# A pair pass on a grid of 128 edges, with the attributes laid out turned

## The chip, the cores and the metric

The kernel runs on one core of one Trainium2 chip. The metric is the device time of one launch in microseconds, as the median of several runs. Beside it there is one profiled execution, from which all rows below are taken.

## The reference, cut to what matters

Four graph layers run one after another on a graph of N = 6250 nodes and E = 106250 edges, sorted by destination; the width is D = 128. Layers 0 (two graph attentions), 1 and 3 (graph convolutions) are not changed in what they compute. The changed part is mainly layer 2:

```python
pos_e = x_feat[src] + edge_attr
v = jax.nn.gelu(pos_e @ W1.T + b1, approximate=False) * bases
aggr = jax.ops.segment_sum(v, dst, num_segments=n_nodes)
```

`edge_attr` and `bases` are two arrays of 106250 x 128 floats. The kernel computes `pos_e @ W1.T + b1` as a table row `x_feat @ W1.T + b1`, gathered by `src`, plus `edge_attr @ W1.T`.

## The kernel before, in words

The nodes stand in NB = 49 blocks of P = 128 (the partition count). A tile is 128 edges that follow each other in the sorted list. The tile tables (`tile_tables`, L485 to L656) give each block as many tiles as its edges fill, rounded up: a block's first tile begins at that block's first edge, so the last tile of a block also reads some edges of the next block, which are masked because their place in the block (`LOCAL`) is 128 or more. The number of tiles is fixed at TILES = 880, in GROUPS = 220 groups of GT = 4. Counted on the input's destination list, 854 tiles have edges of their own; the other 26, at the end, are padding: their edge number is clamped to E, where the padded source list holds zeros, so all 128 rows that such a tile gathers are one and the same row.

Three stages gather by `SRC` for all 880 tiles, one indirect DMA per tile, issued by POOL in `gather` (L1026, recorded under L1033) into a ring of DEEP = 12 groups: the logits of the two attention layers (`gat_logits`) and the pair pass. At the end of each logits stage POOL also issues 16 scatters that add edge weights to an adjacency matrix in DRAM (`merge`, L1114); the first groups of scatters each wait for the landing of the one before. Gathers and scatters use the same POOL queue. Every stage ends with a barrier of all engines, in which POOL drains.

`pair_pass` (L1620) does, per group of 4 tiles: SP fetches 4 x 128 KB of attributes and bases into a ring of 6 groups (L1651, one DMA per tile, starting at the tile's first edge); POOL gathers the 4 x 128 table rows; PE turns the attributes (4 transposes, L1660); ACT copies them from PSUM (L1667); PE multiplies with the weights (L1675); DVE adds the gathered rows (`sum_up`, L1684); ACT applies gelu (L1688); DVE multiplies with the bases (L1694) and builds 4 one-hot matrices (L1045); PE multiplies one-hot and values (L1708); DVE adds 4 products, each to its block of the accumulator (L1063). All PSUM buffers are pairs, the value ring V has 4 places. The order of the instructions on each engine is that of the list in `pipeline`, which says how many groups a piece runs behind the gather: products 4, additions 5. Each engine works through its list in order; semaphores tie them.

In `sort_edges` (L284) SP loads the destination list twice to SBUF and copies the source, destination and weight lists inside DRAM, each as one flat transfer (L301); the copies must be there only at the end of that stage. In `tile_tables` a chain of small DVE operations computes where each tile begins; when it is known POOL fetches 21 windows of edges (L588), and DVE turns them into masks and keys.

## Time and profile before

| what | value |
|---|---|
| median of 3 runs | 6823.73 us (6820.1 to 6828.18) |
| the profiled execution's own time | 6820.84 us |
| its span in the trace | 6819.0 us |
| mean granted TensorE clock | 0.843 |
| pair pass, first gather to next stage | 4237 to 5370 us |
| first logits stage, gathers | 161 to 1285 us |
| second logits stage, gathers | 2001 to 3125 us |

Engines are PE (matmul), PEld (its weight loads), DVE, ACT, POOL and SP. A row of a group of instructions gives the count, the busy time, the mean duration of one and the idle time of the engine just before them with what ended it; "issue" is a wait that the profile shows no releaser for. Times in a timeline are from the start of the span.

### The profile page before, as it was taken

What the parts mean: (1) busy time and instruction counts of PE and PEld (TensorE: products, weight loads), DVE (VectorE), ACT (ScalarE), POOL (GpSimd) and SP (SyncE); (2) the same over time, 40 slices, a digit from 0 to 9 for tenths busy, and PEclk for the clock granted to TensorE, in tenths of its full rate; (3) what the DMA queues carried; (4) which work ended last, traced back from release to release, by engine and by line L of the source; (5) the groups of instructions that cost most, each with busy time, mean ns of one, the idle gap of its engine ahead of it and who ended that gap; (6) DMA issues with size and microseconds to landing.
All of it is one profiled execution on the core that took longest, in us unless ns stands there. A gap on an engine that the chain in (4) does not pass through costs nothing. (4 is left out here: it accounts for less than half of the span.)

```text
span 6819.0 us, 113163 instructions
## 1 busy us (share of the span) xinstructions
PE 5493.8 (81%) x30494; PEld 4417.2 (65%) x30494; DVE 3783.5 (55%) x13003; ACT 2171.3 (32%) x7007; POOL 4607.1 (68%) x4391
## 2 busy tenths in 40 slices
PE   2988998538769999885886996666666699999998
PEld 2777787536667777774775995665666455555555
DVE  6555562288975555223887445666666644344343
ACT  4333334268943333333995003222222300000000
POOL 1777677678857777777886661777777267276473
PEclk9777678678967777876997998888888799999999
DMA  6888875656734444335444884555555489899997
GB/s 217 256 276 277 261 214 160 116 104 138 142 68 102 105 103 105 80 80 54 77 76 117 287 288 139 165 157 157 158 158 157 79 289 307 287 305 299 302 304 256
DMA packets 903995, 1231.39 MB, mean 181 GB/s; under 512 B 230601, under 2 KB 640861, under 8 KB 890407
## 3 DMA queue, kind: packets, MB, share of 16 engines
q1 hardware_dynamic: 607544, 887.00, 41.0%
q0 software_dynamic: 207392, 219.55, 17.9%
q10 hardware_dynamic: 88428, 117.57, 5.1%
q8 instruction: 256, 4.19, 0.3%
q14 instruction: 375, 3.07, 0.1%
HBM read 987.45 MB, written 237.38 MB: 180 GB/s over the span
## 5 line engine op out<-in xcount | busy, mean ns | idle before, releaser
L1033 POOL DMA_INDIRECT ACC<-table,TABS x1760 | 1696.9, 964 | 628.2 <-issue 603.0
L1348 POOL DMA_INDIRECT BUF<-table,TABS x840 | 799.3, 952 | 581.6 <-issue 245.6
L1114 POOL DMA_INDIRECT adjacency<-TABS x600 | 966.9, 1612 | 311.5 <-issue 260.2
L1033 POOL DMA_INDIRECT BUF<-table,TABS x880 | 841.5, 956 | 331.5 <-issue 331.5
L1805 PE MATMUL picked<-ident,ACC 128*128 128x128 f32 (+1 forms) x3520 | 890.7, 345 | 0.0
L1804 PE MATMUL picked<-G,OH 128*128 128x128 f32 (+1 forms) x2352 | 619.6, 356 | 203.9 <-DMA ACC<-table,TABS 110.8
L2185 PE MATMUL asum<-BUF 128*128 128x144 f32 x3520 | 561.2, 305 | 165.6 <-DVE BUF L2163 162.6
L1805 PEld LDWEIGHTS picked<-ident,ACC 128*128 128x128 f32 (+1 forms) x3520 | 673.2, 222 | 0.0
L1804 PEld LDWEIGHTS picked<-G,OH 128*128 128x128 f32 (+1 forms) x2352 | 431.6, 218 | 342.1 <-issue 315.8
L1708 PE MATMUL sums<-BUF,G 128*128 128x128 f32 x1760 | 320.0, 339 | 399.0 <-DVE ACC L1063 398.7
L2185 PEld LDWEIGHTS asum<-BUF 128*128 128x128 f32 x3520 | 476.4, 197 | 196.4 <-issue 182.1
L1825 PEld LDWEIGHTS lcol<-attT,BUF 128*128 128x128 f32 (+1 forms) x3520 | 539.3, 232 | 55.7 <-issue 49.8
L2131 ACT ACTIVATE BUF<-iota_row,TABS 128x128 f32<-128x128 f32 x1760 | 555.1, 386 | 23.5 <-PEq L89 23.5
L1708 PEld LDWEIGHTS sums<-BUF,G 128*128 128x128 f32 x1760 | 277.7, 240 | 435.5 <-issue 435.2
L1825 PE MATMUL lcol<-attT,BUF 128*128 128x8 f32 (+1 forms) x3520 | 545.7, 278 | 2.7 <-ACT BUF L1843 2.7
L1817 DVE TENSOR_TENSOR BUF<-BUF,picked 128x512 f32<-128x512 f32 (+1 forms) x440 | 298.0, 678 | 406.1 <-ACT BUF L1811 404.9
L1063 DVE TENSOR_TENSOR ACC<-ACC,asum 128x144 f32 (+1 forms) x1760 | 462.7, 263 | 94.3 <-PE asum L2185 14.4
L1881 DVE SCALAR_TENSOR_TENSOR BUF<-BUF,TABS,wspread 128x128 bf16<-128x128 f32 (+1 forms) x600 | 324.4, 541 | 337.7 <-PE wspread L1864 234.3
L1831 ACT ACTIVATE ACC<-lcol 128x32 f32<-128x32 f32 (+1 forms) x440 | 81.7, 186 | 1281.5 <-PE lcol L1825 1272.8
L1783 DVE TENSOR_SCALAR G<-BUF,iota_col 128x512 f32<-128x512 bf16 x440 | 223.5, 509 | 478.6 <-DMA BUF<-locals 476.1
L1688 ACT ACTIVATE BUF<-BUF 128x512 f32<-128x512 f32 x220 | 138.6, 630 | 837.3 <-DVE BUF L1684 837.3
L1262 PE MATMUL sums<-ACC,BUF 128*128 128x128 f32 x3332 | 386.1, 276 | 23.3 <-DMA BUF<-adjacency 13.5
(397 smaller groups left out, 10318.8 us busy)
## 6 DMA issues: line engine op xcount, KB each, us to landing
TABS<-adjacency SPq DMA_DIRECT2D x272, 512.0 KB
BUF<-in_edge_pair SPq DMA_DIRECT2D x880, 128.0 KB
BUF<-adjacency SPq DMA_DIRECT2D x102, 1024.0 KB
BUF<-adjacency SPq DMA_DIRECT2D x204, 512.0 KB
adjacency<-zeros ACTq DMA_DIRECT2D x44, 1792.0 KB
G<-adjacency SPq DMA_DIRECT2D x136, 512.0 KB
kept<-ACC SPq DMA_DIRECT2D x220, 272.0 KB
G<-kept SPq DMA_DIRECT2D x220, 272.0 KB
```

The lines of the kernel that those rows point to most:

```text
L1033: po.indirect_dma_start(rows[:, slot, j, 0:width], None, tab, bass.IndirectOffsetOnAxis(ap=SRC[:, q * GT + j:q * GT + j + 1], axis=0)).the ...
L1063: ve.tensor_tensor(at, at, self.from_[:, j, 0:self.width], ALU.add).then_inc(S("added"), 1)
L1114: po.indirect_dma_start(adj_flat, bass.IndirectOffsetOnAxis(ap=PLACE[:, k:k + 1], axis=0), TOTAL[:, k:k + 1], None, compute_op=ALU.add).th ...
L1262: m = pe.matmul(sums[:, j, 0:P], RA[n % len(RA)][:, (i * w + j) * P:(i * w + j + 1) * P], xw[:, b + i, :], start=b + i == 0, stop=b + i == ...
L1348: po.indirect_dma_start(R[:, q % deep_ring, j, :], None, table, bass.IndirectOffsetOnAxis(ap=SRC[:, k:k + 1], axis=0)).then_inc(S(f"gather ...
L1708: m = pe.matmul(sums[h][:, j, :], HOTS[:, slot, j, :], V[:, q % 4, j, :], start=True, stop=True)
L1804: pe.matmul(z, XRB[q % 3][:, j, :], OHT[:, slot, j, :], start=True, stop=False)
L1805: m = pe.matmul(z, R[:, q % DEEP, j, :], ident[:, :], start=False, stop=True)
L1825: m = pe.matmul(lcol[slot % 2][:, j * H:(j + 1) * H], Z[:, q % 3, j * P:(j + 1) * P], attT[0:W, 0:H], start=True, stop=True)
L1881: ve.scalar_tensor_tensor(JUNK[:, at % 3, 0:j + 1, :], KEYS[:, n % 2, 0:j + 1, :], KEY[:, k:k + 1], wspread[:, 0:j + 1, :], ALU.is_equal, ...
L2131: ac.activation(HOT[:, slot, j, :], iota_row[:, :], ACT.Abs, scale=-1.0, bias=LOCAL[:, bass.ds(q * GT + j, 1)]).then_inc(S("gap"), 1)
L2185: m = pe.matmul(sums[slot % 2][:, j, 0:WIDE], HOT[:, slot, j, :], RHS[:, slot, j, :], start=True, stop=True)
```

## The change

1. Tiles lie on a grid: the edge list is cut into 831 cells of 128 edges, and each block gets all the cells that hold any of its edges. A cell that two blocks share appears twice, and the edges of the other block are masked, now on both sides (`LOCAL` below 0 or 128 and more). Counted on the same list, 879 of the 880 tiles have edges of their own. The loops still run over 880 tiles and 220 groups. `START` holds a cell number rather than an edge number.
2. The attribute array is laid out on the host per cell, turned to 128 features x 128 edges. The pair pass no longer turns it: `turn_attr` and `copy_attr` are gone, and `times_w` reads the fetched tile.
3. The pair pass has deeper rings: 9 groups of fetched pairs (6 before), 6 of values (4), 4 PSUM buffers each for `pre` and `sums` (2). The order is written out: sums run 4 groups behind the gather, the multiplication with the bases 5, products 6, additions 9. One-hots and additions alternate on DVE.
4. The three edge lists are copied as 128 rows of equal length each; they are padded to a multiple of 128.
5. The tile tables need more small DVE operations, and the masks of the keys and of the adjacency places (`put_aside`) one more each.
6. The path for unsorted edges (not taken here, the list is sorted) turns and turns back the attributes.

```diff
-TAIL = 2 * P
+SPREAD = 834
+TAIL = SPREAD * P - FRONT - E
 GT = 4
 RING = 4
 DEEP = 12
 SORT_T = -(-E // P)
+CELLS = SORT_T + 1
...
-                sp.dma_start(copy, given).then_inc(S("edges_copied"), 16)
+                sp.dma_start(copy.rearrange("(p c) -> p c", p=P), given.rearrange("(p c) -> p c", p=P)
+                             ).then_inc(S("edges_copied"), 16)
...
-            go(ve, lambda: ve.tensor_tensor(number[:, 0:NB], starts[:, 1:NB + 1], starts_t, ALU.subtract))
-            go(ve, lambda: ve.tensor_scalar(number[:, 0:NB], number[:, 0:NB], float(P - 1), None, ALU.add))
-            go(ve, lambda: ve.tensor_copy(number_i, number[:, 0:NB]))
-            go(ve, lambda: ve.tensor_scalar(number_i, number_i, 7, None, ALU.logical_shift_right))
-            go(ve, lambda: ve.tensor_copy(number[:, 0:NB], number_i))
+
+            def first_cell(cell, edges, plus):
+
+                go(ve, lambda: ve.tensor_scalar(number_i, edges, float(plus), None, ALU.add))
+                go(ve, lambda: ve.tensor_scalar(number_i, number_i, 7, None, ALU.logical_shift_right))
+                go(ve, lambda: ve.tensor_copy(cell, number_i))
+
+            first_cell(first, starts_t, 0)
+            first_cell(shift, starts[:, 1:NB + 1], P - 1)
+            go(ve, lambda: ve.tensor_tensor(shift, shift, first, ALU.subtract))
+            go(ve, lambda: ve.tensor_tensor(filled, starts[:, 1:NB + 1], starts_t, ALU.is_gt))
+            go(ve, lambda: ve.tensor_tensor(number[:, 0:NB], shift, filled, ALU.mult))
...
-            go(ve, lambda: ve.scalar_tensor_tensor(shift, first, float(-P), starts_t, ALU.mult, ALU.add))
+            first_cell(shift, starts_t, 0)
+            go(ve, lambda: ve.tensor_tensor(shift, shift, first, ALU.subtract))
+            go(ve, lambda: ve.tensor_scalar(shift, shift, float(P), None, ALU.mult))
...
+            go(ve, lambda: ve.tensor_scalar(cell, edge, 1.0 / P, None, ALU.mult))
...
-            go(ve, lambda: ve.tensor_scalar(real_edge, local, float(P), None, ALU.is_lt))
+            go(ve, lambda: ve.tensor_scalar(real_edge, local, 0.0, None, ALU.is_ge))
+            go(ve, lambda: ve.scalar_tensor_tensor(real_edge, local, float(P), real_edge, ALU.is_lt, ALU.mult))
...
-            PD = 6
-
-            rooms = BUF[2][:, :, :].rearrange("p b d -> p (b d)")
-            PAIR = BUF[1][:, 0:2 * PD * GT, :].rearrange("p (r t a) d -> p r t (a d)", r=PD, t=GT)
+            PD, VD, FREE = 9, 6, 4
+            SUM_LATE, BASE_LATE, PRODUCT_LATE, ADD_LATE = 4, 5, 6, 9
+
+            V = BUF[2][:, 0:VD * GT, :].rearrange("p (r t) d -> p r t d", r=VD)
+            halves_of_pairs = [BUF[1][:, 2 * GT * i:2 * GT * (i + 1), :] for i in range(PD - 3)]
+            halves_of_pairs += [BUF[2][:, VD * GT + 2 * GT * i:VD * GT + 2 * GT * (i + 1), :] for i in range(3)]
+            PAIR = [h.rearrange("p (t a) d -> p t (a d)", a=2) for h in halves_of_pairs]
             R = BUF[0][:, 0:DEEP * GT, :].rearrange("p (r t) d -> p r t d", r=DEEP)
-            EAT = rooms[:, 0:2 * GT * P].rearrange("p (r t d) -> p r t d", r=2, t=GT)
-            V = rooms[:, 2 * GT * P:6 * GT * P].rearrange("p (r t d) -> p r t d", r=4, t=GT)
-            HOTS = G[:, :, :, :].rearrange("p r t d -> p (r t d)")[:, 0:4 * GT * P].rearrange(
+            four = G[:, :, :, :].rearrange("p r t d -> p (r t d)")[:, 0:4 * GT * P].rearrange(
                 "p (r t e) -> p r t e", r=4, t=GT)
+            HOTS = [four[:, i] for i in range(4)] + [OH[:, i] for i in range(2)]
+            assert len(HOTS) == VD
...
-                turned = [psum(ps, f"turned{i}", [P, GT, P]) for i in range(2)]
-                pre = [psum(ps, f"pre{i}", [P, GT, P]) for i in range(2)]
-                sums = [psum(ps, f"sums{i}", [P, GT, P]) for i in range(2)]
-                adder = Adder(acc, sums, D, "v_free")
...
+                pre = [psum(ps, f"pre{i}", [P, GT, P]) for i in range(FREE)]
+                sums = [psum(ps, f"sums{i}", [P, GT, P]) for i in range(FREE)]
...
+                    cells = pairs.rearrange("(c p) d -> c p d", p=P)
                     for q in range(GROUPS):
                         at = nc.values_load_multi_w_load_instructions(
-                            START[0:1, bass.ds(q * GT, GT)], engines=(SP,), min_val=0, max_val=E,
-                            skip_runtime_bounds_check_because="a tile's first edge is a minimum with E")[1]
+                            START[0:1, bass.ds(q * GT, GT)], engines=(SP,), min_val=0, max_val=CELLS - 1,
+                            skip_runtime_bounds_check_because="a tile's cell is a minimum with the last one")[1]
                         wait(sp, S("based"), q - PD + 1)
                         settle(sp, "sync")
                         for j in range(GT):
-                            sp.dma_start(PAIR[:, q % PD, j, :], pairs[bass.ds(at[j], P), :]
+                            sp.dma_start(PAIR[q % PD][:, j, :], cells[bass.ds(at[j], 1), :, :].rearrange("a p d -> p (a d)")
                                          ).then_inc(S(f"pair{q % PD}"), 16)
...
-                def turn_attr(q, slot, turn):
-                    h = slot % 2
+                def times_w(q, slot, turn):
                     pe.wait_ge(S(f"pair{q % PD}"), 16 * GT * (q // PD + 1))
 
-                    wait(pe, S("attr_copied"), q - 1)
+                    wait(pe, S("summed"), q - FREE + 1)
                     for j in range(GT):
-                        m = pe.transpose(turned[h][:, j, :], PAIR[:, q % PD, j, 0:D], ident[:, :])
-                    m.then_inc(S("attr_turned"), 1)
-
-                def copy_attr(q, slot, turn):
-                    h = slot % 2
-                    ac.wait_ge(S("attr_turned"), q + 1)
-                    wait(ac, S("pre_done"), q - 1)
-                    ac.activation(EAT[:, h], turned[h][:, :, :], ACT.Copy).then_inc(S("attr_copied"), 1)
-
-                def times_w(q, slot, turn):
-                    h = slot % 2
-                    pe.wait_ge(S("attr_copied"), q + 1)
-
-                    wait(pe, S("summed"), q - 1)
-                    for j in range(GT):
-                        m = pe.matmul(pre[h][:, j, :], EAT[:, h, j, :], wmat[:, :], start=True, stop=True)
+                        m = pe.matmul(pre[q % FREE][:, j, :], PAIR[q % PD][:, j, 0:D], wmat[:, :], start=True, stop=True)
                     m.then_inc(S("pre_done"), 1)
...
-                def hots(q, slot, turn):
-                    wait(ve, S("v_free"), q - 3)
-                    for j in range(GT):
-                        m = one_hot(HOTS[:, slot], q * GT, j)
-                    m.then_inc(S("hot"), 1)
+                    ve.tensor_tensor(v, v, PAIR[q % PD][:, :, D:2 * D], ALU.mult).then_inc(S("based"), 1)
+
+                def hot(q, j):
+                    if not 0 <= q < GROUPS:
+                        return
+                    if not j:
+                        wait(ve, S("v_free"), q - VD + 1)
+                    m = one_hot(HOTS[q % VD], q * GT, j)
+                    if j == GT - 1:
+                        m.then_inc(S("hot"), 1)
 
                 def products(q, slot, turn):
-                    h = slot % 2
                     pe.wait_ge(S("hot"), q + 1)
                     pe.wait_ge(S("based"), q + 1)
-                    wait(pe, S("added"), (q - 1) * GT)
+                    wait(pe, S("added"), (q - FREE + 1) * GT)
                     for j in range(GT):
-                        m = pe.matmul(sums[h][:, j, :], HOTS[:, slot, j, :], V[:, q % 4, j, :], start=True, stop=True)
+                        m = pe.matmul(sums[q % FREE][:, j, :], HOTS[q % VD][:, j, :], V[:, q % VD, j, :], start=True, stop=True)
                     m.then_inc(S("v_free"), 1)
 
-                def add(q, slot, turn):
-                    adder.start(q, slot)
+                def add_and_hots(u):
+
+                    q = u - ADD_LATE
+                    if q >= 0:
+                        ve.wait_ge(S("v_free"), q + 1)
+                        blocks = blocks_of(DVE, q)
                     for j in range(GT):
-                        adder.tile(j)
+                        hot(u - BASE_LATE, j)
+                        if q >= 0:
+                            wait(ve, S("added"), q * GT + j)
+                            at = acc[:, bass.ds(blocks[j], 1), :].rearrange("p a d -> p (a d)")
+                            ve.tensor_tensor(at, at, sums[q % FREE][:, j, :], ALU.add).then_inc(S("added"), 1)
...
-                pipeline(nc, [(gather_rows, 0), (turn_attr, 1), (copy_attr, 1),
-                              (times_w, 2), (times_base, 3), (sum_up, 2), (gelu, 2), (hots, 2), (products, 4),
-                              (add, 5)])
+                for u in range(GROUPS + ADD_LATE):
+                    for piece, late in ((gather_rows, 0), (times_w, 1), (add_and_hots, 0), (sum_up, SUM_LATE),
+                                        (gelu, SUM_LATE), (times_base, BASE_LATE), (products, PRODUCT_LATE)):
+                        q = u - late
+                        if piece is add_and_hots:
+                            add_and_hots(u)
+                        elif 0 <= q < GROUPS:
+                            piece(q, q % RING, q // RING)
...
+                    ve.scalar_tensor_tensor(LATER[:, cols], LOCAL[:, cols], 0.0, LATER[:, cols],
+                                            ALU.is_lt, ALU.add).then_inc(S("aside"), 1)
...
-    inputs["edge_pair"] = np.concatenate([inputs.pop("edge_attr_128"), inputs.pop("edge_attr_128_n2")], axis=1)
+    attr, base = (np.pad(np.asarray(inputs.pop(name)), ((0, CELLS * P - E), (0, 0))).reshape(CELLS, P, D)
+                  for name in ("edge_attr_128", "edge_attr_128_n2"))
+    inputs["edge_pair"] = np.concatenate([attr.transpose(0, 2, 1), base], axis=2).reshape(CELLS * P, 2 * D)
```

## Rows read from the trace of the kernel before

**Rows 1.** The page, part 1: busy time, share, instructions.

```profile
...
PE 5493.8 (81%) x30494; PEld 4417.2 (65%) x30494; DVE 3783.5 (55%) x13003; ACT 2171.3 (32%) x7007; POOL 4607.1 (68%) x4391
```

**Rows 2.** Groups of instructions (busy, mean ns, idle before) of the pair pass, 4230 to 5370.

```profile
...
L1033 POOL DMA_INDIRECT BUF<-table,TABS x880 | 841.5, 956 | 331.5 <-issue 331.5
L1708 PE MATMUL sums<-BUF,G 128*128 128x128 f32 x1760 | 320.0, 339 | 399.0 <-DVE ACC L1063 398.7
L1675 PE MATMUL pre<-wmat,BUF 128*128 128x128 f32 x1760 | 303.3, 330 | 0.0
...
L1063 DVE TENSOR_TENSOR ACC<-ACC,sums 128x128 f32 x880 | 250.5, 285 | 97.0 <-DVE ACC L1063 3.3 <-PE sums L1708 0.6
L1045 DVE TENSOR_SCALAR G<-iota_row,TABS 128x128 f32<-128x128 f32 x880 | 192.6, 290 | 0.0
L1660 PE MATMUL turned<-ident,BUF 128*128 128x128 f32 x880 | 177.4, 339 | 33.2 <-DMA BUF<-in_edge_pair 33.1
L1684 DVE TENSOR_TENSOR BUF<-pre,BUF 128x512 f32<-128x512 f32 x220 | 152.1, 691 | 348.4 <-issue 279.3 <-PE pre L1675 57.5 <-DMA BUF<-table,TABS 10.9
L1694 DVE TENSOR_TENSOR BUF<-BUF 128x512 f32<-128x512 f32 x220 | 150.7, 685 | 0.7 <-issue 0.7
...
L1667 ACT ACTIVATE BUF<-turned 128x512 f32<-128x512 f32 x220 | 128.1, 582 | 54.1 <-PE turned L1660 53.4
```

**Rows 3.** Line 1033 over the whole span: ns min/median/max, first and last start.

```profile
...
L1033 POOL DMA_INDIRECT BUF<-table,TABS x880: 941/947/1347, 4237.0 to 5345.7; - x176
```

**Rows 4.** Timeline (start, us, engine, line, idle before) of the pair pass's end.

```profile
...
5345.69 0.95 POOL L1033 DMA_INDIRECT BUF<-table,TABS  x1 [0.30 <-issue]
...
5359.99 0.69 DVE L1684 TENSOR_TENSOR BUF<-pre,BUF 128x512 f32<-128x512 f32 x1 [1.31 <-issue]
...
5367.77 1.57 DVE L1063 TENSOR_TENSOR ACC<-ACC,sums 128x128 f32 x4 [0.43 <-DVE ACC L1063]
```

**Rows 5.** Line 1033 alone, 5199 to 5311.5, with time from issue to landing.

```profile
...
DMA to landing us min/median/max: 2.8/3.0/3.7
```

**Rows 6.** Line 1033 alone, 5312 to 5370.

```profile
...
L1033 POOL DMA_INDIRECT BUF<-table,TABS x28: 943/947/1319, 5311.2 to 5345.7; - x28
...
DMA to landing us min/median/max: 13.4/14.0/14.2
```

**Rows 7.** POOL's timeline, end of the first logits stage.

```profile
...
1284.18 0.94 POOL L1033 DMA_INDIRECT ACC<-table,TABS  x1 [0.31 <-issue]
1285.42 1.63 POOL L1114 DMA_INDIRECT adjacency<-TABS  x1 [0.30 <-issue]
...
1303.80 1.57 POOL L1114 DMA_INDIRECT adjacency<-TABS  x1 [11.15 <-DMA adjacency<-TABS]
...
1313.70 1.55 POOL L1114 DMA_INDIRECT adjacency<-TABS  x1 [2.74 <-issue]
...
1326.71 1.55 POOL L1114 DMA_INDIRECT adjacency<-TABS  x1 [0.30 <-issue]
```

**Rows 8.** POOL's timeline, end of the second logits stage.

```profile
...
3142.29 1.56 POOL L1114 DMA_INDIRECT adjacency<-TABS  x1 [2.06 <-DMA adjacency<-TABS]
```

**Rows 9.** DVE's timeline at the start of the tile tables.

```profile
...
48.96 0.21 DVE L504 TENSOR_TENSOR st<-st 128x49 f32<-128x49 f32 x1 [1.99 <-PEq L345]
49.21 0.19 DVE L505 TENSOR_SCALAR st<-st 128x49 f32<-128x49 f32 x1
```

**Rows 10.** DVE's timeline behind the edge windows.

```profile
...
94.24 0.64 DVE L595 CAST BUF<-BUF 128x910 f32<-128x910 int32 x1 [12.03 <-DMA BUF<-w_sorted,st]
...
107.54 1.09 DVE L619 SCALAR_TENSOR_TENSOR BUF<-BUF 128x896 f32<-128x896 f32 x1
```

**Rows 11.** Line 1893, the mask of `put_aside`.

```profile
...
L1893 DVE SCALAR_TENSOR_TENSOR TABS<-TABS x2: 435/460/486, 1024.1 to 2744.1; 128x320 f32<-128x320 f32 x1, 128x280 f32<-128x280 f32 x1
```

**Rows 12.** SP's waits, first 48 us (us in total, times, longest).

```profile
...
SPq L235 <- DVE FLAG L338: 12.7, 1, 12.7
```

**Rows 13.** POOL's groups in the second logits stage, 1995 to 3125.3.

```profile
...
L1033 POOL DMA_INDIRECT ACC<-table,TABS x880 | 856.4, 973 | 272.5 <-issue 272.5
```

More of the change, by code:

```diff
@@ L544, in tile_tables @@
             placed = st[0][:, 88:88 + TCOL]
+            cell = st[0][:, 96:96 + TCOL]
+            go(ve, lambda: ve.tensor_scalar(cell, edge, 1.0 / P, None, ALU.mult))
             go(ve, lambda: ve.tensor_scalar(scaled, blk, turn_by[:, :], None, ALU.add))
@@ L555, in tile_tables @@
                 rows = psum(ps, "rows", [1, 2, 1024])
-                for n, (col, tab) in enumerate(((blk, BLOCK), (edge, START))):
+                for n, (col, tab) in enumerate(((blk, BLOCK), (cell, START))):
                     for g in range(TCOL):
```

37 lines of the change are left out of this document (23 added, 14 removed).

## The prediction

> **What bounds the kernel now.** The page comes first: no engine is full over the span, the longest are PE at 81% and POOL at 68% [rows 1]. These are means over stages with different limits, so the change has to be read in its own stages. The largest part of it is the pair pass, and there the groups of instructions decide. DVE, PE and ACT all stand idle in it for hundreds of microseconds. POOL is the one engine that never waits for anybody: its 880 gathers take 841.5 us, and all of its idle time is "issue", 331.5 us, about 0.3 us before each [rows 2]. From the first gather at 4237.0 [rows 3] to the start of the last at 5345.69 [rows 4] lie 1108.7 us, over 879 steps 1.261 us each, or 5.05 us per group of four. DVE waits 348.4 us in front of `sum_up`, 279.3 of it under "issue" [rows 2]; a gather lands 3.0 us after its issue [rows 5], and I read this wait as the wait for the gathered rows. So this pass runs at the pace at which POOL issues.
>
> The next view is the same line in two windows. Up to 5311 a gather lands in 2.8 to 3.7 us [rows 5]; behind that in 13.4 to 14.2 us [rows 6]. The input's list gives 854 tiles with edges of their own and 26 padding tiles, whose 128 rows are one and the same row. 26 x 1.261 = 33 us before the last gather is 5313, just where landing turns slow. I take the repeated row as the cause. What follows is in the timeline: the last gather is issued at 5345.69, but its `sum_up` runs at 5359.99 and the last four additions end at 5367.77 + 1.57 = 5369.3 [rows 4]. The last timelines are those of the logits stages, which gather by the same table. There POOL goes on to scatters as soon as its gathers are issued, and its second group of scatters waits 11.15 us for the first to land, behind the slow gathers in the same queue; with ordinary landing that wait is like the next one, 2.74 us [rows 7]. In the second attention layer 2.06 us are lost the same way [rows 8].
>
> **The change, part by part.**
>
> *Transposes and copies removed.* PE is busy 320.0 + 303.3 + 177.4 = 800.7 us over 220 groups, 3.64 us per group; without the 880 transposes 2.83. ACT loses 220 copies of 0.58 us [rows 2]. Both are below POOL's 5.05 us already, so in the steady part this is worth 0. The cover is POOL's issue; were it gone, the 128.1 us of copies and 177.4 us of transposes would be the price. What is late next is the gather, as before.
>
> *DVE's new order.* A group costs 4 additions of 0.285, 4 one-hots of 0.29, 0.691 and 0.685 [rows 2]: 3.68 us at most, the same work as before. Interleaved, each addition's wait for the one before it falls behind a one-hot. 3.68 is under 5.05: worth 0 in the steady part. Behind the waiting `sum_up` on DVE now stand the bases of the group before, and the additions of a group 5 further back; with 6 places for values and 4 buffers of PSUM nobody is blocked by that.
>
> *Deeper fetch ring.* SP may run 9 groups ahead. At the start that is 36 transfers instead of 24, beside gathers that have 12 groups of room: 0.
>
> *The drain of the pair pass.* With 879 real tiles the last gather should land like those of [rows 5]: 5345.69 + 3.0 = 5348.7. `sum_up` of the last group can then start, as PE is groups ahead. Behind it DVE has, in program order: 0.69; the additions of group 215 with the last one-hots between them, 4 x (0.285 + 0.29) = 2.3; the bases, 0.69; and the additions of groups 216 to 219. Four additions in a row take 1.57 [rows 4]; with 0.3 for the register loads and waits ahead of them (estimate; the wait in that row is 0.43) 1.87 each, 7.5 in all. Sum 11.2, end at 5359.9 against 5369.3: **-9.4 us**. Bounds: 0 if the landing stays slow; -12 if the additions follow without gaps and the rows are there 1.4 us sooner.
>
> *First logits stage.* POOL's chain from 1284.18 to the last scatter (1326.71 + 1.55) sets the end, with the drain of the barrier. The wait of 11.15 becomes about 2.74 [rows 7]: **-8.4 us**. Bounds: 0, and -10.9 if it shrinks to the 0.3 of the other scatters.
>
> *Second logits stage.* 2.06 - 0.3 [rows 8]: **-1.8 us**, bounds 0 and -1.8.
>
> *Tile tables.* Ahead of the windows the DVE chain has 9 operations in place of 5, and then 5 in place of 1: 8 more. One takes 0.19 to 0.21 us, and the next starts 0.25 behind [rows 9]: 8 x 0.23 = +1.8, all on the path, for POOL's window fetch starts behind them and DVE then waits for the windows (12.03 us, [rows 10]). Behind the windows one more operation over 128x896, 1.09 us [rows 10], in a chain with no gaps: +1.1. Together **+2.9**, bounds +2 and +4. The new `cell` operation and the shift of START lie beside POOL's windows: 0.
>
> *Mask in `put_aside`.* Two more operations of 0.46 us, at about 1024 and 2744 [rows 11], in stages that POOL's gathers pace and hundreds of microseconds before anybody waits for them: 0, at most +0.9.
>
> *Edge lists as equal rows.* SP's own wait at the end of that stage is for DVE, 12.7 us [rows 12]; the copies are issued some 40 us earlier. Their form can only move the landing of the two loads issued ahead of them: 0, bounds -2 and +2.
>
> *Grid in the other stages.* The loops still have 880 tiles; 25 more gather real rows instead of one row, 25 fewer scatter nothing but padding. Outside the three stages above nothing waits on these: 0, bounds -3 and +3. (The first logits stage has waits on its `kept` ring that may fall otherwise.)
>
> Sum: -9.4 - 8.4 - 1.8 + 2.9 = -16.7 us. Against the profiled execution's own 6820.84 that gives 6804.1; the median of the runs shown, 6823.73, lies 2.9 above it, and the median is what is asked for: **6807 us**, -0.25%.
>
> *A rule that speaks against it.* POOL's gathers in the pair pass last 0.941 to 1.347 us, their mean is 0.956 against a median of 0.947 [rows 2, 3]: something stretches a few of them. The Trainium skill (SBUF — State Buffer, "Who interferes with whom") says that DVE and GpSimd share a port pair which one of them holds for a whole instruction, that `tensor_scalar` can take it in its two-port modes, and that POOL's descriptor writing is then locked out. The one-hots are such instructions, and the change spreads them over more of DVE's time. By that rule the sum would be worse; by the row, in which 880 one-hots at 0.29 us already lie beside the gathers, the cost is 9 ns a gather. It is the second rival below, priced from rows.
>
> **The rivals.**
>
> 1. *The slow landing is not the padding's doing* (it comes, say, with the end of a list, and stays). For: the trace shows when, not why. Against: it starts where the padding starts, in all three stages that gather by this table [rows 6, 7, 8]. Then the last rows are there at about 5359.7, the drain behind them takes 11.2, the pair pass ends 1.6 later than now, and the waits of the logits stages stay: 6823.7 + 2.9 + 1.6 = 6828.
> 2. *One-hots between the additions stretch POOL's gathers.* Place: the pair pass; price: 880 times the growth of the mean; it decides from 16.7/880 = 19 ns on, a mean of 975 instead of 956. The gathers of the second logits stage, beside other DVE work, have 973 [rows 13], so such a mean occurs. At 1.00 us it would be +38.7: 6807 + 39 = 6846, slower than before. Against: number, shapes and durations of DVE's operations in the pass are the same as now.
> 3. *Only the pair pass gains* (the scatters of the first logits stage wait for something else, such as the zero fill of the adjacency or each other): 6807 + 8.4 + 1.8 = 6817. For: the wait is named after the scatters' own landing. Against: the next one in the row is 2.74 only.
> 4. *The pair pass was paced by the loop over PE, ACT and DVE, and POOL's constant 0.3 hides that*: then 5.05 us per group would fall to about 4.2, 220 x 0.85 = 187 us less, 6620. Against: the ring of 12 groups would have to be full and POOL's waits would show a releaser and vary; they do not.
>
> **How the numbers follow.** Forecast 0.65; rival 1 0.12; rival 2 0.08; rival 3 0.12; rival 4 0.03. Between the forecast's own bounds (each term's bounds taken together as unlikely to fall on one side at once) it lies at 6797 to 6816. Two executions of this kernel differ by up to 8 us, 0.1%; 0.2%, 13.6 us, is about what a measurement can tell from no change, so "faster" means below 6810.1. Of the forecast's 0.65 some four fifths lie there, 0.51, and rival 4's 0.03: 0.54. Slower by over 0.2% is rival 2, 0.08. Within 0.2% is what is left, the upper fifth of the forecast's range and rivals 1 and 3: 0.38. The range takes in the forecast's bounds and rival 3, and stops short of rivals 1, 2 and 4: 6795 to 6822.
>
> **What the new profile would show.** Right: POOL's gathers in the pair pass still 1.25 to 1.27 us apart with 0.3 of "issue" before each; landing near 3 us to the end in all three gathering stages; last `sum_up` about 3 us behind the last gather; about 11 us from there to the end of the pass; the first wait of the second group of scatters 2 to 3 us; PE less busy in the pair pass by some 180 us with no effect on its length; the first gather of the first logits stage about 3 us later than now. Wrong: landings of 14 us at the end (rival 1), a mean gather over 975 ns (rival 2), a wait of 11 us before the fifth scatter (rival 3), or gathers of the pair pass closer than 1.25 us (rival 4).

## The result and the profile after

The changed kernel takes 6840.73 us (median of 20 runs, 6825.09 to 6865.56), the kernel before 6826.02 us beside it (20 runs, 6811.87 to 6844.63). The ratio is 1.0022, with an interval of 1.0013 to 1.0031. It is slower by 9 to 21 us, where -16.7 us were forecast. The profiled execution took 6833.4 us, its span is 6831.6, against 6819.0. Two executions of one kernel differ by more than the 8 us that the prediction took from three of them: the 20 of the kernel before spread over 33 us.

The gathers of the pair pass show where. First the same groups as in [rows 2] (busy us, mean ns, idle before), 4210 to 5384 of the changed kernel:

```profile
L1060 POOL DMA_INDIRECT BUF<-table,TABS x880 | 885.5, 1006 | 331.4 <-issue 331.4
...
L1736 DVE TENSOR_TENSOR ACC<-ACC,sums 128x128 f32 x880 | 250.7, 285 | 4.1 <-issue 1.4 <-DVE ACC L1736 0.8
...
L1696 DVE TENSOR_TENSOR BUF<-pre,BUF 128x512 f32<-128x512 f32 x220 | 152.1, 692 | 509.9 <-DMA BUF<-table,TABS 478.3 <-PE pre L1688 19.1 <-PE sums L1722 9.3
L1706 DVE TENSOR_TENSOR BUF<-BUF 128x512 f32<-128x512 f32 x220 | 150.9, 686 | 0.0
```

L1060 is the gather (L1033 before), L1696 `sum_up` (L1684), L1706 `times_base`, the multiplication by the bases (L1694), L1736 the additions (L1063). POOL still waits for nobody: the idle time under "issue" is what it was, 331.4 us. But a gather lasts 1006 ns on the mean, in place of 956: 44.0 us over 880. The line alone over the whole span, to be set against [rows 3]:

```profile
L1060 POOL DMA_INDIRECT BUF<-table,TABS x880: 941/947/1466, 4216.2 to 5368.8; - x176
```

The median is 947 ns in both. So not every gather got slower, some did by much: 135 are over 1.1 us, 17 before. From the first gather to the last are 1152.6 us, 1108.7 before: +43.9. The pair pass begins 20.8 us earlier and its last gather starts 23.1 us later.

(Below, a gather that `times_base` lengthens is called held.) A timeline from the middle of the pass (start, duration, engine, line, idle before) shows one long gather and what lies beside it:

```profile
4739.90 0.69 DVE L1696 TENSOR_TENSOR BUF<-pre,BUF 128x512 f32<-128x512 f32 x1 [2.40 <-DMA BUF<-table,TABS]
4740.51 0.68 DVE L1706 TENSOR_TENSOR BUF<-BUF 128x512 f32<-128x512 f32 x1
...
4740.70 1.31 POOL L1060 DMA_INDIRECT BUF<-table,TABS  x1 [0.30 <-issue]
4741.11 0.28 DVE L1072 TENSOR_SCALAR G<-iota_row,TABS 128x128 f32<-128x128 f32 x1
...
4742.31 0.94 POOL L1060 DMA_INDIRECT BUF<-table,TABS  x1 [0.30 <-issue]
4743.56 0.95 POOL L1060 DMA_INDIRECT BUF<-table,TABS  x1 [0.30 <-issue]
```

`times_base` starts at 4740.51, the gather 0.19 us later, and it lasts 1.31 us. The three gathers that follow lie beside one-hots and additions and last 0.94 and 0.95. I sorted all 880 by the time from the start of the last `times_base` to their own start:

```
                       0-100   100-200  200-300  300-400  400-500 ns  all others
changed: gathers          39        62       27       17        4         731
         mean ns        1309      1356     1261     1162     1053         947
before:  gathers           0         5        8        3       10         854
         mean ns           -      1325     1257     1120     1062         950
```

All 135 long gathers are in the first five columns, in which 149 start; before, all 17, and 26 start there. From 100 ns on, the later a gather starts in `times_base` the shorter it is, one for one: a long gather ends 1.50 us behind the start of that instruction, 0.82 behind its end. (In the first column 29 of the 39 are long.) 142 of the 149 are third gathers of their group. The reason is in the new order. `times_base` now stands directly behind `sum_up`, and `sum_up` is released by the fourth gather's landing (the wait of 478.3 us in the group above); 0.6 us later `times_base` starts, and POOL's next gather, the third of the following group, starts 0.72 us behind `sum_up` at the median. POOL and DVE beat in one rhythm, so this meeting repeats in about two groups of three. Before, `times_base` stood ahead of `sum_up`, 2.88 us behind the last one, between two starts.

The other terms came. The timelines of the ends, for [rows 7] and [rows 4] (first POOL at the end of the first logits stage, then POOL's last gather of the pair pass, then DVE behind it):

```profile
1284.10 0.94 POOL L1060 DMA_INDIRECT ACC<-table,TABS  x1 [0.30 <-issue]
...
1294.69 1.57 POOL L1141 DMA_INDIRECT adjacency<-TABS  x1 [2.12 <-DMA adjacency<-TABS]
...
1304.15 1.55 POOL L1141 DMA_INDIRECT adjacency<-TABS  x1 [2.30 <-issue]
...
1317.16 1.55 POOL L1141 DMA_INDIRECT adjacency<-TABS  x1 [0.30 <-issue]
```

```profile
5368.80 0.94 POOL L1060 DMA_INDIRECT BUF<-table,TABS  x1 [0.30 <-issue]
```

```profile
5372.85 0.69 DVE L1696 TENSOR_TENSOR BUF<-pre,BUF 128x512 f32<-128x512 f32 x1 [3.55 <-DMA BUF<-table,TABS]
...
5382.02 1.58 DVE L1736 TENSOR_TENSOR ACC<-ACC,sums 128x128 f32 x4 [0.25 <-DVE ACC L1736]
```

The last gathers of the pass, 5335 to 5395, against [rows 6]:

```profile
L1060 POOL DMA_INDIRECT BUF<-table,TABS x28: 943/947/1024, 5334.9 to 5368.8; - x28
...
DMA to landing us min/median/max: 2.5/2.5/2.6
```

The landing of 14 us is gone, and with it the wait of 11.15 us behind the first group of scatters (now 2.12).

### The profile page after: what moved, and what is told of

Its sections match the earlier page's. It is cut to its first block and busy times, and to the rows that moved or that the text cites. A ratio compares the mean times of both kernels' runs of the same rounds, so it can differ in the third digit from the quotient of the medians.

```text
span 6831.6 us, 110756 instructions
## 1 busy us (share of the span) xinstructions
PE 5435.8 (80%) x29614; PEld 4345.1 (64%) x29614; DVE 3749.6 (55%) x13015; ACT 2060.7 (30%) x6787; POOL 4653.3 (68%) x4391
## 3 DMA queue, kind: packets, MB, share of 16 engines
q0 software_dynamic: 207392, 219.55, 16.6%
## 5 line engine op out<-in xcount | busy, mean ns | idle before, releaser
L1060 POOL DMA_INDIRECT ACC<-table,TABS x1760 | 1697.1, 964 | 626.5 <-issue 602.5
L1375 POOL DMA_INDIRECT BUF<-table,TABS x840 | 799.7, 952 | 573.2 <-issue 247.1
L1060 POOL DMA_INDIRECT BUF<-table,TABS x880 | 885.5, 1006 | 331.4 <-issue 331.4
L1688 PE MATMUL pre<-wmat,BUF 128*128 128x128 f32 x1760 | 360.2, 369 | 497.7 <-DVE BUF L1696 463.3
L2215 PE MATMUL asum<-BUF 128*128 128x144 f32 x3520 | 547.1, 299 | 170.6 <-DVE BUF L2193 167.7
L1688 PEld LDWEIGHTS pre<-wmat,BUF 128*128 128x128 f32 x1760 | 310.5, 265 | 545.1 <-issue 508.8
L1696 DVE TENSOR_TENSOR BUF<-pre,BUF 128x512 f32<-128x512 f32 x220 | 152.1, 692 | 509.9 <-DMA BUF<-table,TABS 478.3
```

The lines of the kernel that those rows point to most:

```text
L1060: po.indirect_dma_start(rows[:, slot, j, 0:width], None, tab, bass.IndirectOffsetOnAxis(ap=SRC[:, q * GT + j:q * GT + j + 1], axis=0)).the ...
L1375: po.indirect_dma_start(R[:, q % deep_ring, j, :], None, table, bass.IndirectOffsetOnAxis(ap=SRC[:, k:k + 1], axis=0)).then_inc(S(f"gather ...
L1688: m = pe.matmul(pre[q % FREE][:, j, :], PAIR[q % PD][:, j, 0:D], wmat[:, :], start=True, stop=True)
L2215: m = pe.matmul(sums[slot % 2][:, j, 0:WIDE], HOT[:, slot, j, :], RHS[:, slot, j, :], start=True, stop=True)
```

## The experiments

Theory B: a gather that starts in the first half microsecond of `times_base` is held until that instruction ends; the change put `times_base` where a gather mostly starts. Rival H is the rival 2 of the prediction: the one-hots between the additions. A further rival is that rings, layout or grid do it. Last, the granted clock is 0.831 in the profile of the changed kernel and 0.843 in that of before; runs 1 and 4 have 0.831 as well and are faster than the kernel before, so the clock doesn't make the loss.

The runs fell on two kinds of chip. On the first kind (two chips) the kernel before takes 6827 to 6833 us beside the runs, on the second kind (three others) 8166 to 8169. Only on the first kind does POOL set the pace of the pair pass (section 9), so only there does a time speak of the loss. Ratios are always to the kernel before, measured beside the run. In the edits, "..." marks what is left out.

Runs 1 to 4 are on the first kind.

### 1. `times_base` in the middle of the one-hots and additions (changed kernel)

```
-    ... (gelu, SUM_LATE), (times_base, BASE_LATE), (products, PRODUCT_LATE)):
+    ... (gelu, SUM_LATE), (products, PRODUCT_LATE)):
...
     for j in range(GT):
+        if j == 2 and 0 <= u - BASE_LATE - 1 < GROUPS:
+            times_base(u - BASE_LATE - 1, 0, 0)
         hot(u - BASE_LATE, j)
```

> The changed kernel, with one edit: the multiplication by the bases no longer follows sum_up directly but stands between the second and the third pair of one-hot and addition, some 0.8 us later. Theory B (a gather that starts in the first half microsecond of the multiplication is held up by it; in the changed kernel the third gather of a group always does): the multiplication now starts 1.4 us behind sum_up, where no gather starts; mean gather of the pair pass 945 to 955 ns instead of 1006, time 6841 - 880 x 0.053 = 6794 us (6788 to 6802). Rival H (one-hots between the additions stretch the gathers): the one-hots alternate as before, mean stays 1000 to 1010 ns, 6841 us.

Measured: 6802.6 us, ratio to before 0.9974 (0.9963 to 0.9985). The gathers, as the page has them:

```profile
L1060 POOL DMA_INDIRECT BUF<-table,TABS x880 | 843.2, 958 | 331.3 <-issue 331.3
```

48 ns less, and nothing else was moved. Mean and time are just above what I expected (by 3 ns and 0.6 us): the phase moves with the edit, and 52 gathers still start in the first 500 ns of `times_base`, 26 of them at 400 to 500 where the hold is 0.12 us. All 27 over 1.1 us are among the 52. B holds, H falls as the cause of the loss: the alternation is unchanged.

### 2. One-hots and additions in blocks again (changed kernel)

```
     for j in range(GT):
         hot(u - BASE_LATE, j)
+    for j in range(GT):
         if q >= 0:
             wait(ve, S("added"), q * GT + j)
```

> The changed kernel with the four one-hots in a row and then the four additions in a row, as in the kernel before; the multiplication by the bases stays directly behind sum_up. Theory B: nothing changes, mean gather 1000 to 1010 ns, 6838 to 6846 us. Rival H: mean gather back to 956 ns, 6797 us.

Measured: 6840.06 us, ratio 1.0018 (1.0004 to 1.0032).

```profile
L1060 POOL DMA_INDIRECT BUF<-table,TABS x880 | 883.8, 1004 | 331.3 <-issue 331.3
```

Again 149 gathers in the first 500 ns, 132 over 1.1 us. The alternation is worth nothing, either way, as the prediction had it.

### 3. `times_base` inside the one-hots (kernel before)

```
     for j in range(GT):
+        if j == 2 and q > 0:
+            times_base(q - 1, 0, 0)
         m = one_hot(HOTS[:, slot], q * GT, j)
     ...
+    if q == GROUPS - 1:
+        times_base(q, 0, 0)
...
-    (times_w, 2), (times_base, 3), (sum_up, 2), ...
+    (times_w, 2), (sum_up, 2), ...
```

> The kernel before, with one edit: the multiplication by the bases stands between the second and the third one-hot behind sum_up, instead of ahead of sum_up. Theory B: it then starts 1.0 us behind the start of sum_up, and the third gather of a group starts at 1.16 us: held up, mean gather 990 to 1015 ns instead of 956, time 6826 + 880 x 0.045 = 6866 us (6850 to 6880). Rival H: no one-hot stands between additions, mean 956, 6826 us.

Measured: 6828.18 us, ratio 1.0004 (0.9991 to 1.0016); mean gather 954 ns. A miss, and H's number. The trace shows why: with `times_base` no longer ahead of it, `sum_up` starts at another point of POOL's rhythm. The third gather starts 0.73 us behind `sum_up` at the median, not 1.17, so ahead of `times_base` at 1.0. Only 7 gathers start in its first 500 ns. A gather that starts ahead of it isn't held (in the changed kernel 24 gathers start within 100 ns ahead of it, with a mean of 946 ns); the one exception that I found is here, a gather that starts 0.14 us ahead of it at 4264.45 and lasts 1.65 us. I had taken the phase for fixed, and it moves with the edit. The trace also shows that H's mechanism exists, though it is small: 245 other gathers start in the first 200 ns of a one-hot here, with a mean of 969 ns, against 944 of those that start beside additions. That is about 6 us over the pass, and most of why the mean is 954 with almost nothing held. It also says where `times_base` must stand for a hold: at 0.6. That is run 9.

### 4. The same place and length, but one operand in PSUM (changed kernel)

```
-    ac.activation(V[:, q % VD], V[:, q % VD], ACT.Gelu)
+    ac.activation(pre[q % FREE][:, :, :], V[:, q % VD], ACT.Gelu)
-    ve.tensor_tensor(v, v, PAIR[q % PD][:, :, D:2 * D], ALU.mult)
+    ve.tensor_tensor(v, pre[q % FREE][:, :, :], PAIR[q % PD][:, :, D:2 * D], ALU.mult)
     ... # and times_w waits for "based" of q - FREE in place of "summed"
```

> The changed kernel, in its own order, but the gelu is written to PSUM, so that the multiplication by the bases reads one operand from PSUM and one from SBUF; same length, same place, same result. Theory B in its narrow form (it is the two operands in SBUF that hold a gather up): mean gather about 946 ns, time 6841 - 880 x 0.060 = 6788 us (6780 to 6798). Theory B in its wide form (any DVE instruction of 0.68 us in this place does): stays at 1000 to 1010 ns, 6841 us. Rival H: also 1000 to 1010 ns, 6841 us.

Measured: 6794.2 us, ratio 0.9962 (0.9947 to 0.9977).

```profile
L1060 POOL DMA_INDIRECT BUF<-table,TABS x880 | 831.3, 945 | 331.4 <-issue 331.4
```

```profile
4742.39 0.68 DVE L1706 TENSOR_TENSOR BUF<-pre,BUF 128x512 f32<-128x512 f32 x1
```

`times_base` is as long as it was, 0.68 us, and directly behind `sum_up`; 111 gathers start in its first 500 ns, with a mean of 944 ns, and none of the 880 is over 1.02 us. So it is not any DVE instruction of this length in this place that holds them: with both operands in SBUF it does, with one in PSUM it doesn't. (The edit also moves the gelu's output out of SBUF; run 1 leaves the gelu as it was and loses the holds by the place alone.) `sum_up` reads a pair of PSUM and SBUF as well, and holds none: in the changed kernel 37 gathers start in its first 500 ns, the longest of 948 ns.

### 5. `times_base` as four instructions (changed kernel)

```
-    ve.tensor_tensor(v, v, PAIR[q % PD][:, :, D:2 * D], ALU.mult)
+    for j in range(GT):
+        m = ve.tensor_tensor(v[:, j], v[:, j], PAIR[q % PD][:, j, D:2 * D], ALU.mult)
     ...
```

> The changed kernel, with the multiplication by the bases in its place but as four instructions over 128x128 instead of one over 128x512, all with both operands in SBUF. If a gather is held until the instruction ends that runs when it starts, the longest hold is a quarter as long: gathers of 1.0 to 1.2 us in place of 1.3 to 1.45, mean 950 to 975 ns, 6841 - 880 x 0.045 = 6801 us (6792 to 6815). If it is held until DVE has no such instruction left, the mean stays at 1000 ns or more, 6841 us.

The second and the third run of it:

> The changed kernel with the multiplication by the bases as four instructions over 128x128, once more, for the same reason. Held until the instruction ends: gathers of 1.0 to 1.2 us at most, mean 950 to 975 ns, 6801 us (6792 to 6815). Held until DVE has no such instruction left: mean 1000 ns or more, 6841 us.

> The changed kernel with the multiplication by the bases as four instructions. In the two runs on the other chip no gather was over 1.09 us, with a mean of 957 ns. Where POOL paces the pass this gives 6841 - 880 x 0.049 = 6798 us (6790 to 6808); if the holds come more often when the phase locks, up to 6815.

Three runs, all on the second kind of chip: ratios 1.0011 (0.9999 to 1.0023), 1.0003 (0.9992 to 1.0013), 0.9994 (0.9982 to 1.0006) there. Its time says nothing (below), its gathers do. From the second run, the timeline and the line's min/median/max:

```profile
5523.58 0.89 DVE L1707 TENSOR_TENSOR BUF<-BUF 128x128 f32<-128x128 f32 x4
...
5524.02 1.08 POOL L1060 DMA_INDIRECT BUF<-table,TABS  x1 [0.30 <-DVE BUF L1696]
```

```profile
L1060 POOL DMA_INDIRECT BUF<-table,TABS x880: 942/947/1085, 5096.7 to 6482.7; - x176
```

In none of the three is a gather over 1.09 us, though 190 to 200 start within 500 ns behind the start of one of the four; the means are 957, 957 and 950 ns, as expected. That holds do occur on this kind of chip is shown by run 6. The gather above starts in the third of the four instructions (each of 0.28 us; they start at 5523.58, 5523.78, 5523.98 and 5524.19) and ends 0.83 us behind that one's end, as the long ones of the changed kernel do. A gather is held to the end of the one instruction that runs when it starts and then goes on, though another follows.

### 6. The padding's rows made different (kernel before)

```
+            if name == "src":
+                a[-tail:] = np.arange(tail) * 37 % N
```

> The kernel before, in whose padding of the list of source rows 256 different rows stand instead of row 0 256 times; nothing else is changed. If the repeated row is what makes the last gathers land in 14 us, they now land in about 3: behind the last gather the pair pass ends 9 us sooner, the first logits stage 9 us, the second 2 us: 6827 - 20 = 6807 us (6802 to 6812). If the slow landing comes with the end of a list, 6827 us.

The second to the fourth run of it:

> The kernel before with 256 different rows in the padding of the list of sources, once more, for the same reason. On a chip like the first: landing of the last gathers about 3 us, pair pass, first and second logits stage end 9, 9 and 2 us sooner behind their last gather, 6827 - 20 = 6807 us (6802 to 6812); if the slow landing comes with the end of a list, 6827 us.

> The kernel before with 256 different rows in the padding. Where POOL paces the gathers: from the last gather to the end of the stage 9 us less in the pair pass and in the first logits stage, 2 us less in the second, 6807 us (6802 to 6812); if the repeated row is not the cause, 6827 us.

> The kernel before with 256 different rows in the padding. Where the kernel before takes 6827 to 6833 us: from the last gather to the end of the stage 9 us less in the pair pass and in the first logits stage, 2 us less in the second, 20 us in all, 0.3% (0.2 to 0.4%). If the repeated row is not the cause, no difference.

All four runs of it fell on the second kind of chip: ratios 0.9985 (0.9974 to 0.9997), 0.9967 (0.9954 to 0.998), 0.9988 (0.9974 to 1.0002), 0.9971 (0.9955 to 0.9988). Their mean is 0.9978, -18 us of 8166.

The traces settle what rival 1 of the prediction left open. Gathers move their rows on queue q0. Here is what its packets did in the 14 us that begin 0.7 us behind the start of the last gather (packets, MB, share of the 16 engines), first with the old padding (run 9, third time), then with this one (its fourth run):

```profile
q0 software_dynamic: 209, 0.40, 58.2%
```

```profile
q0 software_dynamic: 44, 0.07, 1.9%
```

In the four profiles with this padding the last of these packets starts 2.2 to 2.6 us behind the last gather, in four with the old padding on the same kind of chip (`times_base` moved, or the gelu in PSUM) 12.3 to 14.4. So the repeated row is what makes the last gathers land late, and not the end of a list.

What this is worth is less clear. From the last gather to the end of the pair pass are 46.8 to 51.7 us here, against 54.3 to 56.1 in those four: some 7 us. From the last gather to the end of POOL's drain in the first logits stage nothing differs (41.8 to 42.9 and 41.5 to 43.2), nor in the second. So the padding alone makes the kernel faster, but on this kind of chip I can place less than half of it, and on the first kind it wasn't run alone.

### 7. and 8. Beside each other on the first kind of chip: the changed kernel, and run 4 again

> The changed kernel itself, beside the next runs. On a chip on which the kernel before takes 6827 us: 6841 us, mean gather 1006 ns. On one on which it takes 8168 us the landing of the rows paces the pair pass, so that holds cost nothing and the padding, the logits stages and the drain still gain: 8168 - 15 = 8153 us (8140 to 8170).

> The version with the gelu in PSUM. Where POOL paces the pair pass: 6794 us again. Where landing paces it: like the changed kernel itself, 8153 us (8140 to 8170), with a mean gather of 944 to 947 ns; nothing over 1.1 us.

Measured: changed 6844.92 us, ratio 1.0013 (0.9998 to 1.0028), mean gather 996; 137 start in the first 500 ns of `times_base`, 116 are over 1.1 us. With the gelu in PSUM 6786.26 us (4 executions), ratio 0.993 (0.9904 to 0.9956), mean 945, none over 1.05. This version beats the kernel before in both of its comparisons, and the changed kernel here, where both ran side by side.

The kernel before with the gelu in PSUM ran on the second kind of chip alone:

> The kernel before, with the gelu written to PSUM, so that the multiplication by the bases reads only one operand from SBUF. Theory B: the 26 gathers that it holds now are held no more, mean 944 to 946 ns instead of 956, 6827 - 880 x 0.011 = 6817 us (6812 to 6824); what is left between it and the changed kernel with the same edit (6794) is then the work of the grid, about 20 us. Against it: with two buffers of PSUM for the products the matrix multiplication waits for the multiplication by the bases, and if that shows, gathers wait and the time is above 6827 us.

Measured: ratio 1.0006 (0.9993 to 1.0019). 71 gathers start in the first 500 ns of `times_base`, their mean is 946 ns, none is over 1.02 us: what run 4 showed, in the other kernel. The time is not the one expected; there POOL waits for `sum_up` in this pass (run 9 below), so its pace alone doesn't decide.

### 9. `times_base` directly behind `sum_up` (kernel before)

```
-    (times_w, 2), (times_base, 3), (sum_up, 2), (gelu, 2), (hots, 2), ...
+    (times_w, 2), (sum_up, 2), (times_base, 3), (gelu, 2), (hots, 2), ...
```

> The kernel before, with one edit: the multiplication by the bases stands directly behind sum_up instead of directly ahead of it, its place in the changed kernel. In the run with this multiplication 1.0 us behind the start of sum_up (mean 954 ns) the third gather of a group started 0.72 us behind that start, ahead of the multiplication, so it was not held. Theory B: with the multiplication at 0.61 us the third gather now starts 0.1 us into it and is held to its end; mean 995 to 1015 ns, time 6827 + 880 x 0.049 = 6870 us (6855 to 6880). Rival H, and the rival that the changed kernel's layout or rings do it: mean 954 to 958 ns, 6827 us.

The second to the fourth run of it:

> The kernel before with the multiplication by the bases directly behind sum_up, once more: the first time it ran on a chip on which the kernel before takes 8166 us and the pair pass is paced by the landing of the rows (POOL waits there for sum_up), which says nothing of POOL's pace. On a chip like the first, theory B: the third gather of a group starts some 0.1 us into the multiplication and is held to its end; mean 995 to 1015 ns, +40 us (6855 to 6880). Rivals (alternation, layout, rings): mean 954 to 958 ns, 6827 us.

> The kernel before with the multiplication by the bases directly behind sum_up, on a third chip if it may be. Where POOL paces the pair pass: theory B, mean gather 995 to 1015 ns, 6855 to 6880 us; rivals (alternation, layout, rings), 954 to 958 ns, 6827 us. If the gathers start in front of the multiplication, as in the run with it 1.0 us behind the start of sum_up, theory B gives 955 ns too: what decides is how many start in its first 500 ns.

> The kernel before with the multiplication directly behind sum_up. Where POOL paces the pass: theory B 6855 to 6880 us and a mean gather of 995 to 1015 ns, rivals 6827 us and 956 ns. Where landing paces it: 8168 us, and no more than 10 gathers over 1.1 us, as in the earlier runs there.

The fourth run, on the first kind of chip: 6873.63 us, ratio 1.0053 (1.0034 to 1.0072).

```profile
L1033 POOL DMA_INDIRECT BUF<-table,TABS x880 | 878.1, 998 | 331.2 <-issue 331.2
```

```profile
5017.37 0.68 DVE L1694 TENSOR_TENSOR BUF<-BUF 128x512 f32<-128x512 f32 x1
5017.47 1.41 POOL L1033 DMA_INDIRECT BUF<-table,TABS  x1 [0.30 <-issue]
```

139 gathers start in the first 500 ns of `times_base`, 118 are over 1.1 us, and the kernel before is 40 us slower by one exchange of two entries in a list, inside the 6855 to 6880 us expected. Nothing of the new grid, the rings, the attributes laid out turned or the alternation is in it. That is the whole effect seen in the changed kernel, made alone.

The first three, on the second kind of chip, gave ratios 0.9995 (0.998 to 1.0009), 0.9999 (0.9987 to 1.0011) and 1.0004 (0.9992 to 1.0016). One group and one answer on waits, 5080 to 6500 and 5110 to 6470 of the first of them:

```profile
L1033 POOL DMA_INDIRECT BUF<-table,TABS x880 | 841.5, 956 | 585.2 <-issue 303.6 <-DVE BUF L1684 281.6
```

```profile
POOL BUF L1033 <- DVE BUF L1684: 281.6, 117, 10.1
```

There POOL waits 281.6 us for `sum_up`, which is to say for room in its ring of 12 groups; on the first kind it never does. The exchange also makes no holds there: only 6, 8 and 8 gathers start in the first 500 ns. And where there are holds, they cost nothing that shows: in the four runs of run 6, 95 to 113 gathers start there, with means of 980 to 991 ns, and from the first gather to the last are 1362 to 1369 us, against 1361 to 1367 in these three. What `sum_up` waits for on those chips is put down to transfers and to PE in turn, and I did not settle it.

## Why the prediction was wrong

- *The step that failed is "DVE's new order: worth 0 in the steady part".* It measured +43.9 us. The sum had DVE's work (3.68 us in a group of 5.05) and who waits behind whom, and both are right: DVE still stands idle for hundreds of microseconds (509.9 in front of `sum_up`) and POOL waits for nobody. It left out at what moment of POOL's rhythm each DVE instruction now runs. It even names the new place ("Behind the waiting `sum_up` on DVE now stand the bases of the group before"), but asks there only who is blocked in the order of the list, and the move of `times_base` got no term of its own.
- *Rival 2* had the place (POOL's gathers in the pair pass), the point of decision (a mean of 975 ns) and about the price (6846 us at a mean of 1.00 us; by its own rule 6851 at the 1.006 measured, and 6840.7 came). Its culprit was wrong: run 2 has no one-hot between additions and the same holds. That its number came so near is luck. With a chance of 0.08 it was far too low. The maximum of 1347 ns in [rows 3] against a median of 947 was seen, and taken as 9 ns of a mean. Some 6 us of it over the pass were 26 gathers that start in the first 500 ns of one instruction, 17 of them held 0.15 to 0.4 us; had I looked at which, the term would have been in the sum. Some 3 us more were one-hots (197 gathers start in the first 200 ns of one, with a mean of 961 ns).
- *The rule.* The Trainium skill (SBUF — State Buffer, "Who interferes with whom") says that a DVE instruction with two inputs in SBUF contends with GpSimd instructions that read SBUF, and one with a single input there, outside the two-port modes, does not. I took from that section the part on `tensor_scalar` and its two-port modes. Runs 4 and 9 agree with the part that I left out: holds of up to 0.41 us (the 100-ns means above against 946 ns) with both operands in SBUF, none with one in PSUM. The gather reads its indices from SBUF (TABS in its row), which would make it such a reader; that this read is what waits was not tried. The part that I took shows too, small in this pass (run 3) and larger in the first and second logits stages: there 60 gathers of the kernel before start 100 to 200 ns behind the start of a one-hot over 128x512 (0.51 us), and last 1140 ns on the mean.
- *Transposes and copies removed, deeper ring: 0.* Nothing speaks against it. PE's and ACT's share went and POOL's "issue" stayed at 331.4 us.
- *Drain of the pair pass, -9.4.* From the start of the last gather to the end of the last addition 23.6 us before [rows 4], 14.8 now (5383.60 - 5368.80): -8.8. By its parts: `sum_up` 4.05 us behind the gather where I had 3.0, and 10.75 from there where I had 11.2.
- *First logits stage, -8.4.* From the last gather to the end of the last scatter 44.1 us [rows 7], now 34.6: -9.5, of it 9.03 in the first wait and 0.44 in the second.
- *Second logits stage, -1.8.* The wait is 0.3 us now; the stage behind its last gather takes 37.7 in place of 39.5 us: -1.8.
- *Tile tables, +2.9.* The first window gather starts at 63.8 in place of 62.1, the first gather of the logits stage at 164.3 in place of 160.8: +3.5, inside the bounds.

- *Rival 1's question, the cause of the slow landing.* The prediction took the repeated row for it, and run 6 shows that.
- *Rival 4.* Its 4.2 us per group has no row behind it in the prediction; the chance of 0.03 says how little hangs on it.

These terms give -16.6 us, the forecast to 0.1. That is in part luck: the tile tables cost 0.6 more than their term and the drain gave 0.6 less, while the first logits stage gave 1.1 more.

With +43.9 the terms make +27.3 us, but the spans of the two profiles differ by 12.6 only. So 14.7 us less are in none of them. Laid side by side, the profiles have 9.9 of these between the first logits stage and the gathers of the second (from SP's first load of `heads` to the first gather 665.0 us before, 655.1 after), 3.6 in the gathers of the first logits stage (1123.4 us from first to last before, 1119.8 after), and the rest in pieces of about 1 us. Both stretches scatter by as much with no edit in them: the first is 654.6 to 665.0 us in the six profiles with the new grid on the first kind of chip and 661.4 to 672.0 in the three with the old one, the second 1117.3 to 1133.2 and 1123.4 to 1134.1. Whether a part belongs to the change is open.

The medians say +15 (9 to 21). Two more things scatter. The pair pass's gathers take 1152.6 us in one execution of the changed kernel and 1143.4 in run 7, with 149 and 137 starts in the first 500 ns. And the profile of before was a good one of its kind at the ends: from the last gather's start to the stage's last barrier it took 50.9, 39.5 and 24.4 us in the three stages (the changed one 41.4, 37.7 and 15.5), while runs 3 and 9, with the same grid, took 51.7 to 52.3, 43.5 to 43.8 and 27.6 to 28.0. (In their pair pass `times_base` was moved, which may be part of the 3 us there.) By those the edits gain about 25 us and the account is +10 to +19, around the medians' +15. The forecast of what the edits themselves give was right or a little low: run 1, the change with the gathers' stretch of the kernel before (1110.2 us against 1108.7), is at -0.26% (-0.37 to -0.15), where -0.25% was forecast.

## What to carry to other kernels

Where POOL issues gathers back to back and paces a stage, a long DVE `tensor_tensor` with both operands in SBUF was paid for here by each gather that started in its first 0.5 us; count how many do, and where in a shared rhythm, before moving one. Write one operand to PSUM (here the gelu's output), or cut the instruction up (which shortened the holds; its time was not measured where POOL sets the pace), before looking for a place for it. A maximum far above a median, in a row of the engine that sets the pace, deserves one question: what ran beside it.

## What the runs showed of the hardware

- A gather issued in the first 500 ns of a 0.68 us DVE multiplication with both operands in SBUF lasts up to 1.47 us in place of 0.945; one issued up to 100 ns ahead of it isn't lengthened (946 ns, 24 gathers). With one operand in PSUM: 944 ns, 111 gathers. Cut into four of 0.28 us: at most 1.085 us.
- A gather issued in the first 200 ns of a 0.28 us one-hot (`tensor_scalar`, 128x128) lasts 969 ns on the mean in run 3, one issued beside additions (one operand in PSUM) 944. In the kernel before it is 961 against 946.
- Gathers whose 128 indices are all one row land 13.4 to 17.0 us behind their issue on the first kind of chip (kernel before, run 9), those with different rows at the same place in 2.5 (changed kernel).
- The same programs took 6.8 ms on two chips and 8.2 ms on three others, with granted clocks of 0.83 to 0.84 and 0.77 to 0.79 in the profiles. On the slower kind POOL waits for its ring in the pair pass, and from the first gather to the last lie 1361 to 1386 us in place of 1098 to 1153. The exchange of run 9 cost 0.53% on one kind and nothing that shows on the other.
